# Attended values of four attentions: queries in tiles of 32 as the stationary operand, on one Trainium2 core

## What is computed

```
q, k, v = heads(x @ Wq), heads(context @ Wk), heads(context @ Wv)   # 16 heads, 128 x 16
score = softmax(mask(q @ k.T) / 4)                                  # 128 queries x 128 keys
out = score @ v                                                     # 128 queries x 16
```

## Time and profile before

| | |
|---|---|
| median of three runs | 1673.22 us |
| the profiled execution, as timed | 1673.93 us |
| its span, first to last instruction | 1672.1 us |
| PE busy | 1609.6 us, 96% |
| PE's weight loads busy | 1383.7 us, 83% |
| DVE busy | 1387.7 us, 83% |
| ACT busy | 1073.6 us, 64% |
| POOL busy | 494.2 us, 30% |
| instructions | 61077 |

### The profile page before, as it was taken

One profiled execution on the slowest core, in us unless ns is written; L12 is line 12 of the kernel. 1 busy time (PEld: TensorE's weight loads), 2 busy tenths in 40 slices (PEclk: granted clock), 3 DMA queues, 4 the chain that ended last, 5 costly groups with the idle time before them and its releaser, 6 DMA issues.

```text
span 1672.1 us, 61077 instructions
## 1 busy us (share of the span) xinstructions
PE 1609.6 (96%) x24963; PEld 1383.7 (83%) x24963; DVE 1387.7 (83%) x3587; ACT 1073.6 (64%) x2797; POOL 494.2 (30%) x1256
## 2 busy tenths in 40 slices
PE   7889999999999999999999999999999999999886
PEld 6777888888888888888888888888888888888774
DVE  4588888888888889888888988888898888888552
ACT  2356666766666676666667666666766666676552
POOL 1333223333322332332233233223323322332110
PEclk9999999999999999999999999999999999999997
DMA  6120001000000000000000000000000000000000
GB/s 208 43 81 21 5 19 31 18 25 28 21 2 25 24 25 25 25 22 4 25 24 25 24 24 23 4 24 25 25 24 25 16 10 24 22 28 18 5 5 7
DMA packets 31316, 44.36 MB, mean 27 GB/s; under 512 B 3008, under 2 KB 26176, under 8 KB 30912
## 3 DMA queue, kind: packets, MB, share of 16 engines
q1 hardware_dynamic: 31040, 40.46, 7.6%
HBM read 36.12 MB, written 4.33 MB: 24 GB/s over the span
## 4 chain that ended last, share of the span: by engine, by line
PE 56%; DVE 35%; issue 5%; POOL 2%; DMA 1%; ACT 1%; DVEq 0%; SPq 0%; POOLq 0%; ACTq 0%
PE ring L639 20%; PE ring L645 14%; PE ring L627 6%; DVE conv L1363 5%; DVE maxima_at L1261 5%; PE score L707 4%; DVE decay L1397 3%; PE score L731 3%; PE ring L773 3%; DVE conv L1369 2%; PE ring L858 2%; DVE decay L1401 2%; DVE QB L1272 2%; DVE conv L1358 2%; PE score L671 2%
## 5 line engine op out<-in xcount | busy, mean ns | idle before, releaser
L1538 POOL TENSOR_TENSOR stat<-stat 128x1 f32<-128x1 f32 x224 | 131.7, 594 | 612.8 <-DVE stat L1227 612.3
L1019 ACT COPY actT<-ring 128x256 f32<-128x256 f32 x256 | 95.5, 373 | 264.6 <-PE ring L627 264.2
L1261 DVE TENSOR_REDUCE maxima_at<-score 128x4 f32<-128x512 f32 x388 | 240.8, 684 | 26.0 <-PE score L707 25.2
L1052 ACT ACTIVATE weights<-score 128x512 f32<-128x512 f32 x388 | 200.6, 607 | 28.6 <-PE score L731 28.1
L1363 DVE SCALAR_TENSOR_TENSOR conv<-raw,vectors,conv 128x128 f32<-128x128 f32 x576 | 169.2, 349 | 6.8
L639 PE MATMUL ring<-actT,w_q 128*128 128x128 f32 x1024 | 141.4, 281 | 0.7 <-ACT actT L1019 0.7
L639 PEld LDWEIGHTS ring<-actT,w_q 128*128 128x128 f32 x1024 | 124.5, 191 | 12.8 <-issue 11.3
L639 PE MATMUL ring<-actT,w_up 128*128 128x128 f32 x1024 | 129.1, 280 | 0.5 <-ACT actT L1019 0.5
L639 PEld LDWEIGHTS ring<-actT,w_up 128*128 128x128 f32 x1024 | 120.6, 194 | 3.7 <-ACT actT L1019 1.1
L731 PE MATMUL score<-QB,KE 32*128 32x128 f32 x3104 | 116.7, 286 | 3.8 <-issue 2.8
L1187 ACT ACTIVATE gT<-ring,vectors 128x128 f32<-128x128 f32 x256 | 73.0, 368 | 70.3 <-PE ring L639 69.6
(11 more groups left out here) (179 smaller groups left out, 3809.7 us busy)
## 6 DMA issues: line engine op xcount, KB each, us to landing
decay<-rates_out SPq DMA_DIRECT2D x32, 512.0 KB, 4.1
cT<-in_ctxT SPq DMA_DIRECT2D x32, 128.0 KB, 2.2
x_in<-in_x SPq DMA_DIRECT2D x32, 128.0 KB, 2.5
out<-result SPq DMA_DIRECT2D x32, 128.0 KB, 2.1
row_all<-in_rows SPq DMA_DIRECT2D x1, 1420.0 KB, 10.2
w_in<-in_in_proj SPq DMA_DIRECT2D x1, 1288.0 KB, 6.5
w_k<-in_k SPq DMA_DIRECT2D x4, 256.0 KB, 7.4
w_v<-in_v SPq DMA_DIRECT2D x4, 256.0 KB, 7.2
```

The source lines that it names most:

```text
L1019: nc.scalar.copy(dst.rearrange("p c k -> p (c k)"), t[:, 0:n]).then_inc(read, 1)
L1052: run(weights[:, turned_buffer(it, a_, l), r, :], score[:, r, :], ACT.Exp).then_inc(S["exps"], 1)
L1261: nc.vector.tensor_reduce(maxima_at[:, maxima_buffer(it, a_, l), 32 * r:32 * (r + 1)].rearrange("p (f s) -> p s f", f=2)[:, 0:DC, :], scor ...
L1538: tt(stat[:, l, 10:11], stat[:, l, 2:3], stat[:, l, 4:5], ALU.pow).then_inc(S[done], 1)
```

## The change

`values` swaps the operands. For each head it makes four matmuls, one for each 32 queries: the exponentials of these queries (128 keys by 32) are the stationary operand and the head's values with the column of ones (17 columns) the moving one. The result is tokens by channels at once, 16 x 17 columns of a bank. `attT` and `back` go away, with the buffer `attT` and the spare matmuls before two `back` tasks. `finish` reads the bank of `values`; DVE waits for the three further semaphores `att_full0` to `att_full2` for which ACT waited. All order tables get new numbers.

```diff
-ATT_BUFFERS = 2
...
-SPARE = {("mT0", 0): 11, ("values0", 0): 9, ("back0", 0): 3, ("xhatT", 0): 6, ("ld", 0): 16, ("pairs", 0): 5, ("Y", 0): 18, ("uT", 0): 6, ("xnT", 0): 9, ("ctxT", 0): 10, ("x2T", 0): 7, ("Y", 1): 3, ("mT2", 0): 4, ("back2", 0): 3, ("n3", 0): 3}
+SPARE = {("mT0", 0): 11, ("values0", 0): 9, ("xhatT", 0): 6, ("ld", 0): 16, ("pairs", 0): 5, ("Y", 0): 18, ("uT", 0): 6, ("xnT", 0): 9, ("ctxT", 0): 10, ("x2T", 0): 7, ("Y", 1): 3, ("mT2", 0): 4, ("n3", 0): 3}
...
                 buffer = turned_buffer(it, a_, l)
-                for four in range(H16 // TILES):
-                    for r in range(TILES):
-                        h = TILES * four + r
-                        at = (2 * (h // 8) + h % 2) * P
-                        last = mm(output[ROWS_OF[r], four * P:(four + 1) * P], V2[:, l, h, :],
-                                  weights[:, buffer, h % 8 // 2, at:at + P], start=True, stop=True)
-                        if four == H16 // TILES - 1:
-                            last.then_inc(full if r == TILES - 1 else S[f"att_full{r}"], 1)
-
-            def back(it, a_, l):
-                evacuated(it, f"values{a_}", l, (f"back{a_}", l))
-                flip(it, f"back{a_}", l, attT[:, att_buffer(it, a_, l), :], 4)
+                for h in sorted(range(H16), key=lambda h: h % 8 // 2):
+                    r, at = h % 8 // 2, (2 * (h // 8) + h % 2) * P
+                    for q, queries in enumerate(ROWS_OF):
+                        last = mm(output[queries, h * (DH16 + 1):(h + 1) * (DH16 + 1)],
+                                  weights[:, buffer, r, at + queries.start:at + queries.stop], V2[:, l, h, 0:DH16 + 1],
+                                  start=True, stop=True)
+                        if h == H16 - 1:
+                            last.then_inc(full if q == TILES - 1 else S[f"att_full{q}"], 1)
...
-            def out_turned(it, a_, l):
-                for r in range(TILES - 1):
-                    act.wait_ge(S[f"att_full{r}"], nth_output(it, a_, l))
-                t, read = filled(it, f"values{a_}", l)
-                nc.scalar.copy(attT[:, att_buffer(it, a_, l), :], t[:, :]).then_inc(read, 1)
...
             def weighted(it, a_, l, step, dst):
 
-                t, read = filled(it, f"back{a_}", l)
-                o = t[:, :].rearrange("p (h e) -> p h e", h=H16)
+                for q in range(TILES - 1):
+                    dve.wait_ge(S[f"att_full{q}"], nth_output(it, a_, l))
+                t, read = filled(it, f"values{a_}", l)
+                o = t[:, 0:H16 * (DH16 + 1)].rearrange("p (h e) -> p h e", h=H16)
                 step(nc.vector.reciprocal(rec[:, l, :], o[:, :, DH16]))
                 tt(dst.rearrange("p (h e) -> p h e", h=H16), o[:, :, 0:DH16],
                    rec[:, l, :].unsqueeze(2).broadcast_to((P, H16, DH16)), ALU.mult).then_inc(read, 1)
-                evacuated(it, f"back{a_}", l)
+                evacuated(it, f"values{a_}", l)
```

More of the change, by code:

```diff
@@ L50 @@
 TASKS = dict(
[L51 to L58, removed]
@@ new lines @@
+    mT2=41.1535, mT3=48.8203, mT4=59.3758, n2=41.6618, n3=48.1032, norm2=32.7764, norm3=24.9694, norm4=37.6597, norm5=63.2631,
+    pairs=22.088, proj=27.8878, quads1=31.7066, quads2=38.2035, quads3=47.4731, quads4=58.5177, quadsT2=41.4941,
+    quadsT3=49.7218, quadsT4=62.2347, row=45.8707, scan=14.7577, scores1=32.8557, scores2=34.8034, scores3=47.8021,
+    scores4=68.3936, silu=21.5818, softplus=20.2634, spread=23.5526, store=5.5965, turn1=33.6033, uT=27.4342, up0=67.6101,
+    up1=68.7045, values1=33.8892, values2=42.6448, values3=51.8719, values4=64.6469, x1=15.4992, x1r=14.5543, x2T=36.2299,
@@ new lines @@
+        V2=0.0612, V3=0.2156, Y=0.6654, ctxT=0.1417, exps0=-15.2484, exps2=-7.1153, exps3=39.3094, exps4=39.2861, fc1=0.1978,
+        ld=-0.4972, prep_in=1.3849, row=-0.5701, scores1=-1.1704, silu=-0.685, softplus=-0.929, turn1=-0.3249, uT=0.0348,
+        up0=0.0335, up1=-0.1589, x1=-1.1498, x2T=-0.3494, x3T=-0.5404, x4T=-0.0188, x5T=-0.1681, x6T=-0.1505, xbc0=-0.2503,
+        xbc1=-0.208, xhatT=-0.9967, xnT=-0.4052, z1=-0.1122),
+    DVE=dict(
+        K1=0.8589, K3=0.8413, V4=0.6079, Wo=1.1026, Y=1.4191, conv0=2.1374, conv1=22.9129, decayed=-8.9499, down=1.0519,
+        e2=1.1695, fc2=0.7431, finish0=0.4458, finish1=43.5008, finish2=-0.299, finish3=1.1176, finish4=0.5686, mT0=-0.054,
+        mT2=0.6598, mT3=0.9756, mT4=0.9098, n2=0.4994, n3=0.852, norm2=11.1521, norm3=27.9415, norm4=18.6511, norm5=2.5741,
+        pairs=1.1019, prep_in=-0.5289, prep_masks=17.3958, prep_out=10.7836, prep_q1=-0.3402, proj=0.8544, scan=11.0753,
+        scores0=-0.4084, scores2=6.2997, scores4=-8.6237, silu=0.3801, softplus=-0.2067, uT=0.5774, x1=-1.2533, x1r=0.4207,
+        x3T=-0.3822, xhat=-15.5162, xnT=-0.4384),
@@ L244 @@
            "load_mamba", "load_w1", "load_w2", "load_w3"]
-NO_RING += [f"{task}{a_}" for task in ("quads", "scores", "quadsT", "exps", "attT") for a_ in ATTENTIONS]
+NO_RING += [f"{task}{a_}" for task in ("quads", "scores", "quadsT", "exps") for a_ in ATTENTIONS]
 JOBS = [(what, l, i) for task, l, i in PLACE if task not in NO_RING for what in RING_JOBS.get(task, task).split()]
@@ L376 @@
     before([unit for unit in SCORED if unit[0] != 1], n, MAXIMA_BUFFERS, unit_task("mT"), unit_task("quads"))
-for n in range(ATT_BUFFERS, len(TURNED)):
-    before(TURNED, n, ATT_BUFFERS, unit_task("back"), unit_task("values"))
 for n in range(TURNED_BUFFERS, len(TURNED)):
```

267 lines of the change are left out of this document (120 added, 147 removed).

## The result

The changed kernel takes 1752.18 us, the median of four runs (1748.82 to 1757.15), against 1672.79 us for the kernel before, now the median of four as well. The ratio is 1.0473, with a 95% interval of 1.0436 to 1.0511: it is 79 us slower. The forecast was 1683 us, and its range ended at 1712.

The account below looks back on a forecast made before the run. The prediction took PE's instruction stream to bound the steady part: 1672.1 - 20 (block) - 5 (ends) + 34 (instruction halts) = 1681 us of span, 1683 us with the 1.8 us around it; range 1645 to 1712 us.

Parts of the forecast that it names:

- The bound: Steady part, 200 to 1400 us: PE's instruction stream bounds at 99% busy; DVE at 88% has some 12% to spare.
- The block: values on PE: 1.46 us a unit removed, 1.25 us added, saving 0.21 us a unit, 20 us in all.
- The rule of the Trainium skill: PE matmuls never start closer than about 25 ns: 3.2 us a unit, some 170 us more, 1843 us; 1% chance.
- The halts: PE waiting for instruction packets at the new blocks: 1.6 us at worst, mean 0.37 us a unit, 34 us taken.
- rival B: Instruction halts at the blocks are worse: 2.5 us at the worst edge, 88 us in all, 1737 us; 7% chance.
- 3.8 us: PE's instruction fetch: time from asking for the next packet until it is usable; halts up to 2.5 us.
- The ends: Fill and drain: shorter chain from values to the norm saves 5 us in all, between 2 and 7.
- DVE and the new orders: DVE's added semaphore waits and the new task orders: taken at nothing, the orders within 5 us either way.
- The signs of the forecast: In or right behind PE's blocks: 20 to 50 gaps of 0.5 to 2.5 us ended by "issue" confirm halts.
- A: PE's instructions arrive in time, so no halts at the blocks: 1649 us, faster by 1.5%; 34% chance.
- C: The new form of values is slow on PE: 12.0 ns a pair, 1.54 us a unit, 1697 us; 9% chance.
- D: PE no longer bounds; DVE does or an order is worse, steady PE under 95%: about 1674 us; 7% chance.

Follow-up runs that it names:

- e1: Kernel before with each values matmul cut into four over 32 columns, 128 pairs a unit, old form and orders kept; 1810.9 us.
- e3: Changed kernel with two tiles of 64 queries in place of four of 32, 64 pairs a unit, same orders; 1730.8 us.
- e6: Changed kernel with values computed for even heads only, 34 moving columns, 64 pairs a unit; 1653.0 us.
- e9: Changed kernel with PE's task quadsT3 placed later, behind ld, pairs and x2T; 1797.1 us.
- e2: Kernel before with each values matmul cut into two over 64 columns, 64 pairs a unit; 1669.1 us, ratio 0.9970 to 0.9989.

## Why the prediction was wrong, step by step

**The bound.** Right: PE was the bound, and what changed is when it can issue.

**The block.** Right. 1.25 us a unit was forecast, 1.20 measured at full speed, so that the gain was 25 us in place of 20 forecast. The rule of the Trainium skill that I set aside ("TensorE: Matmul & The Clock Gate", "Wait — 56ns, not 53.3ns?") stayed wrong for this form: 9.4 ns a pair.

**The number of instructions.** Right: 270 packets where 273 were forecast, 33875 pairs for 33887.

**The halts.** This is the step that failed, first by one term, the size at the worst edge. I took 1.6 us "near the two halts seen", a mean of 0.37 us a unit and 34 us in all. Measured are 74 to 76 us more than before, nearly 0.8 us a unit. The largest halt in a block is this one, which loses 2.7 us and is beyond the 2.5 us of rival B:

```profile
1609.46 0.74 PE L749 MATMUL ring<-V,weights 128*32 128x17 f32 x41 [2.64 <-issue]
```

With B's value, put in after the fact, the same working fits what was counted: halts of at most 2.5 us fade over 2.5 / 0.027 = 93 instructions to either side, so 185 of 256 edges, 72%, bring one, with 1.25 us on average. 65 halts for 97 units are 67%, and their mean is 82.8 / 65 = 1.27 us. The fault was in how the 1.6 us were chosen. Two halts in 201 packets show what two edges at chance places cost in blocks that are less dense; they are no estimate of the worst place. The bound from 3.8 us and the block's length stood in the text, worked out from the same rows, and had only 7%.

The 3.8 us behind that bound were themselves read off one halt, and here B's fit is partly luck. The second halt, counted back in the same way, contradicts them: since this line 4 + 64 + 16 + 16 + 14 = 114 pairs, less than a packet's worth, had gone out when PE stopped, and PE went on 5.3 us after it, at 1572.72. By 3.8 us there should have been no halt.

```profile
1567.44 1.13 PE L645 MATMUL ring<-w_v,cT 128*128 128x256 f32 x4
```

The same count for the halts of after that lie inside one line gives 3.5 to 5.6 us for eight in ten. What is steady in them is the part from the transfer's start to PE's next matmul, 2.2 to 2.7 us. When the next transfer is asked for, and why it starts up to 1.5 us after PE has stopped in e1, stays open; 3.8 us less the block's length is no bound.

**The low clock.** It is missing from the sum. 13 us more than before in after, and 30 or more in e1, are lost in stretches at 1.2 GHz, and in both runs every one of those between 150 and 1650 us begins behind a halt. The earlier trace rows showed a mean clock of 1.00, but right behind the halt of the earlier trace rows there was such a stretch, which I had not asked for (the kernel before, granted clock third from the end):

```profile
1570.80:1572.60 1.80, 0.29 (x10) 0.10 (x3) 0.17 (x1) 0.00 (x0) 0.00 (x0) 1.00 0.00 0
1573.60:1580.20 6.60, 5.85 (x50) 3.87 (x54) 2.02 (x6) 2.93 (x7) 0.83 (x2) 0.50 0.01 2
```

**The ends.** Half right. The last unit goes from 1726.16 to DVE's first read in 2.50 us, against 3.93 in the earlier trace rows:

```profile
1726.16 1.91 PE L749 MATMUL ring<-V,weights 128*32 128x17 f32 x128 [2.18 <-issue]
...
1728.66 0.26 DVE L1247 RECIPROCAL rec<-ring 128x16 f32<-128x16 f32 x1 [7.41 <-PE ring L749]
```

1.4 us where 2 to 2.7 were counted for this leg. The block took 1.9 us or so; the mean granted clock over the last 97 us is 0.84. The 5 us in all were not measured by themselves.

**DVE and the new orders.** Taken at nothing within 5 us, while 11 are left for waits in after. They are not the orders' or DVE's by themselves: e3 has the same orders and 2 us left. The argument, that DVE had 12% to spare and PE could win 1% at most by an order, missed what e6 and e9 point to: the pace of an element is also held by chains nearly as tight as PE's own work, so that a gain of PE is lost to them, and a delay is passed on. I wrote that the waits of `rec` for PE would get shorter, since the leg is shorter. They went from 17.5 us in 22 cases to 39.2 us in 43, and I put that down to the halts, which make the blocks late: in e6, with few halts and the same short leg, no wait of `rec` for PE is left in the same stretch (DVE's waits of after, 200 to 1400 us):

```profile
DVE rec L1247 <- PE ring L749: 39.2, 43, 3.2
```

**The rivals.** The signs of the forecast were those seen: gaps in or right behind the blocks ended by "issue", but 65 and not 20 to 50. B had the mechanism and about its size, 88 us for 76 counted, and the low clock and the waits lie on top: 1737 + 13 + 11, less 12 for the smaller halts, is 1749. A and C are excluded by the gaps and by the block's 1.20 us. D is partly there (PE at 94.4% in the steady part), but the gaps are DVE's for 17 us of 67.

**What stays open.** Whether an order exists in which the new form without halts would beat before: every order tried put another wait in the place of the one removed. Also open are when the next packet is asked for and why e2 is 0.2% faster.

## What to carry to other kernels

Count the instructions of a dense block as well as its time: on a PE that is already full, 256 instructions in 1.2 us cost more than the work they saved, while 128 in 1.0 us cost nothing, so that a finer tiling has to be paid for with fewer or longer instructions around it. If a profile of before shows even one gap ended by "issue" inside a task with an instruction packet some 2.5 us ahead of it, weigh a worst case well beyond the halts that chance has shown: the longest seen before lost 1.8 us, those of after 2.7 and those of e1 3.7. In a pipeline whose order is written out by hand, ask what is next late before a gain on the busiest engine is booked: here 20 us of 74 came through.

## What was not expected of the hardware

- The fetch of PE's instructions is visible as a latency: from the start of a packet's transfer to PE's next matmul 2.4 us at 1522.50 and 2.6 us in the earlier trace rows, with no other transfer near in the first of them.
- A halt of some 2 us can be followed by a stretch at 1.2 GHz in which eight matmuls take 1.87 us for 0.99: 8 of 18 in after, 21 of 24 in e1, counting distances of over 1.8 us. In e1 the low clock costs 30 us or more beyond before's.
- In this block a wider stationary tile is dearer than two narrow ones: 31 ns a pair with 64 columns in two tiles, 9.4 ns with 32 in four, the moving side being 17 columns in both. The width and the number of tiles change together, and no run separates them. By that, 64 pairs of the one (1.98 us) take longer than 128 of the other (1.20 us).
